# Causal attention on one core: the transfers of a group's load are issued by GpSimd between the masks of the second and third chunk, and the values have their own semaphore

## The reference

```python
xn = _layernorm(x, axis=-1)
s = _L0_attn_ref(xn, Wq, bq, Wk, bk, Wv, bv, Wo, bo)      # causal attention, the part changed here
g = _silu(_L0_ffn_ref(xn, ...))                           # two layers with windowed attention
x = x + s * g

# in _L0_attn_ref, for a chunk of queries qc of each head:
scores = jnp.einsum('bhqd,bhkd->bhqk', qc, k) * scale
scores = jnp.where(causal_mask[None, None], -jnp.inf, scores)
m = jnp.max(scores, axis=-1, keepdims=True)
p = jax.nn.softmax(scores - m, axis=-1)
oc = jnp.einsum('bhqk,bhkd->bhqd', p, v)
```

## Time and profile before

| | |
|---|---|
| time, median of 3 runs | 4990.12 us (4989.68 to 5007.07) |
| the profiled execution's own time | 4986.53 us |
| its span from first to last instruction | 4984.7 us |
| TensorE clock granted, mean | 0.949 of full speed |
| PE busy | 4590.0 us (92%) |
| DVE busy | 3673.8 us (74%) |
| ACT busy | 2994.0 us (60%) |
| POOL busy | 1342.6 us (27%) |

### The profile page before, as it was taken

How to read it: one execution, slowest core, us unless ns; L and a number is a source line. 1 busy time by engine, 2 the same in 40 slices (tenths; PEclk the granted TensorE clock), 3 DMA queues, 4 the chain that set the end, 5 groups by cost and what they waited for, 6 DMA issues and landing times. The chain is left out here.

```text
span 4984.7 us, 91933 instructions
## 1 busy us (share of the span) xinstructions
PE 4590.0 (92%) x32224; PEld 3005.9 (60%) x32224; DVE 3673.8 (74%) x7585; ACT 2994.0 (60%) x6873; POOL 1342.6 (27%) x1844
## 2 busy tenths in 40 slices
PE   8589999999999996899999999995999999999986
PEld 7433334333334332577777777764677777777766
DVE  7488887887878883777777777754777777777746
ACT  3157776777777774456565666651665656566642
POOL 3112111121111121433333333311433333333300
PEclk9789998999999997899999999996999999999998
DMA  8722432222432222000000000001000000000008
GB/s 300 212 34 35 57 45 36 36 35 41 55 42 36 36 36 69 5 9 18 10 18 10 14 13 14 14 9 65 5 18 10 18 10 18 10 14 14 14 6 277
DMA packets 174917, 214.21 MB, mean 43 GB/s; under 512 B 75068, under 2 KB 126228, under 8 KB 168340
## 3 DMA queue, kind: packets, MB, share of 16 engines
q1 hardware_dynamic: 174484, 208.56, 18.4%
HBM read 124.05 MB, written 83.89 MB: 42 GB/s over the span
## 5 line engine op out<-in xcount | busy, mean ns | idle before, releaser
L601 ACT ACTIVATE a_pt<-a_ring 128x512 f32<-128x512 f32 (+3 forms) x2560 | 1182.8, 542 | 474.4 <-PE a_ring L712 458.8
L652 DVE TENSOR_REDUCE a_mx<-a_ring 128x2 f32<-128x1024 f32 (+3 forms) x1092 | 1129.6, 1064 | 267.9 <-PE a_ring L732 164.3
L996 POOL TENSOR_TENSOR l_rn<-l_ssm,l_half 128x8 f32<-128x8 f32 x256 | 431.7, 1687 | 941.0 <-DVE l_ssm L1278 941.0
L725 PE MATMUL a_ring<-a_ks,a_qs 48*128 48x512 f32 (+3 forms) x2560 | 568.3, 439 | 115.7 <-DMA a_v_in<-v_d 83.1
L712 PE MATMUL a_ring<-a_qs,a_ks 49*128 49x512 f32 (+3 forms) x2560 | 574.3, 456 | 50.8 <-ACT a_pt L601 26.9
L749 PE MATMUL a_ot<-a_pt,a_vt 128*32 128x512 f32 (+3 forms) x5120 | 613.0, 559 | 1.8 <-ACT a_os L607 1.3
L712 PEld LDWEIGHTS a_ring<-a_qs,a_ks 49*128 49x128 f32 x2560 | 255.1, 193 | 454.9 <-ACT a_pt L601 271.8
L1097 ACT ACTIVATE l_pr<-l_pr,l_negm 128x256 f32<-128x256 f32 (+1 forms) x1024 | 501.8, 495 | 6.5 <-DVE l_negm L1330 6.1
L725 PEld LDWEIGHTS a_ring<-a_ks,a_qs 48*128 48x128 f32 x2560 | 265.9, 196 | 380.4 <-ACT a_pt L601 175.7
L575 POOL TENSOR_TENSOR a_gate<-a_gate 128x1 f32<-128x1 f32 x512 | 99.6, 195 | 1413.6 <-ACT a_pt L601 1403.4
L1003 POOL TENSOR_TENSOR l_work<-l_work,l_rot 128x512 f32<-128x512 f32 x256 | 357.4, 1397 | 396.0 <-DVE l_work L1286 396.0
(11 more groups left out here) (173 smaller groups left out, 9070.4 us busy)
## 6 DMA issues: line engine op xcount, KB each, us to landing
qk_d<-p_parts SPq DMA_DIRECT2D x16, 2048.0 KB, 10.4
a_qs<-qk_d SPq DMA_DIRECT2D x96, 256.0 KB, 8.5
a_ks<-qk_d SPq DMA_DIRECT2D x96, 256.0 KB, 18.5
x_d<-l_dx SPq DMA_DIRECT2D x32, 512.0 KB, 2.8
l_xt<-x_d SPq DMA_DIRECT2D x24, 513.0 KB, 3.8
p_x_in<-x SPq DMA_DIRECT2D x16, 512.0 KB, 8.8
x_d<-p_xt SPq DMA_DIRECT2D x16, 512.0 KB, 5.1
v_d<-p_vt SPq DMA_DIRECT2D x16, 512.0 KB, 10.8
```

The source lines that it names most:

```text
L601: act.activation(pt[:, (g * STEPS + s) % NPT, 2 * piece + f, q0:CHUNK], bank("step", g, k, f)[:, q0:CHUNK], ACT.Exp).then_inc(exp_done.sem, 1)
L652: r = dve.tensor_reduce(mx[:, pr, :, t, kc], ring[:, banks[0]:banks[1] + 1, 0:w], AX.X, ALU.max)
L725: mm = pe.matmul(bank("unit", G, n, f)[:, 0:w], qs[rows, v, pr, q0:q0 + P], ks[rows, v, pr, kc * CHUNK:kc * CHUNK + w], start=True, stop=k ...
L996: pool.tensor_tensor(out=rn[:, a * HEADS:(a + 1) * HEADS], in0=ssm[:, a * HEADS:(a + 1) * HEADS], in1=half[:, 0:HEADS], op=ALU.pow).then_i ...
```

## The change

GpSimd issues the 13 transfers instead of SP. They stand in its order between `step` 23 and `step` 24, that is behind the last mask of the second chunk. The transfer into `a_v_in` gets a semaphore of its own, `v_loaded`, for which only `widen` waits; `loaded` now counts the 12 transfers of queries and keys, and PE waits for those alone.

```diff
-        loaded = [tally(f"loaded{u}", 16 * (4 * NSTACK + 1)) for u in range(NSLOT)]
+        loaded = [tally(f"loaded{u}", 16 * 4 * NSTACK) for u in range(NSLOT)]
+        v_loaded = [tally(f"v_loaded{u}", 16) for u in range(NSLOT)]
...
         @block.sync
...
-            def load(G, _):
-                v, b, hg = G % NSLOT, G // NGROUP, G % NGROUP
-                sp.wait_ge(pv_done.sem, pv_done.at(G - NSLOT))
-                for dst, pick, o in ((qs, STACK_Q, 0), (ks, STACK_K, NGROUP)):
-                    for j, s in enumerate(pick):
-                        for f in range(2):
-                            row = f * HALF + j * A_HD
-                            sp.dma_start(dst[row:row + A_HD, v].bitcast(F32), parts_v[s, f, :, hg + o, :, b])\
-                              .then_inc(loaded[v].sem, 16)
-                sp.dma_start(v_in[:, v], v_v[:, b, hg]).then_inc(loaded[v].sem, 16)
...
-                do("row_out", 1); do("row_out", 2); do("load", 1); do("out", -1); do("out", 0); do("row_out", 3)
+                do("row_out", 1); do("row_out", 2); do("out", -1); do("out", 0); do("row_out", 3)
...
         @block.gpsimd
...
+            def load(G, _):
+                v, b, hg = G % NSLOT, G // NGROUP, G % NGROUP
+                pool.wait_ge(pv_done.sem, pv_done.at(G - NSLOT))
+                for dst, pick, o in ((qs, STACK_Q, 0), (ks, STACK_K, NGROUP)):
+                    for j, s in enumerate(pick):
+                        for f in range(2):
+                            row = f * HALF + j * A_HD
+                            pool.dma_start(dst[row:row + A_HD, v].bitcast(F32), parts_v[s, f, :, hg + o, :, b])\
+                              .then_inc(loaded[v].sem, 16)
+                pool.dma_start(v_in[:, v], v_v[:, b, hg]).then_inc(v_loaded[v].sem, 16)
+
             def widen(G, _):
                 v = G % NSLOT
-                pool.wait_ge(loaded[v].sem, loaded[v].per * (G // NSLOT + 1))
+                pool.wait_ge(v_loaded[v].sem, v_loaded[v].per * (G // NSLOT + 1))
...
-                for n in range(0, 49):
+                for n in range(0, 24):
+                    do("step", n)
+                do("load", 1)
+                for n in range(24, 49):
                     do("step", n)
                 do("widen", 1)
```

More of the change, by code:

```diff
@@ L542, in around @@
             def around(do):
-                do("row_out", 1); do("row_out", 2); do("load", 1); do("out", -1); do("out", 0); do("row_out", 3)
+                do("row_out", 1); do("row_out", 2); do("out", -1); do("out", 0); do("row_out", 3)
                 do("row_out", 4); do("out", 1); do("out", 2)
-            program(dict(load=load, row_out=row_out, out=out), around)
+            program(dict(row_out=row_out, out=out), around)
             for t in o_stored:
@@ L585, in around @@
                     do("step", n)
-            program(dict(widen=widen, step=step), around)
+            program(dict(load=load, widen=widen, step=step), around)
         @block.scalar
```

## The result

| | before | changed |
|---|---|---|
| median of 4 runs each | 4994.2 us (4989.7 to 5007.1) | 5184.4 us (5178.7 to 5190.4) |
| ratio, 95% interval | | 1.0386 [1.0361, 1.0411] |
| span of the profiled execution | 4984.7 us | 5188.4 us |
| mean granted clock | 0.949 | 0.930 |

A forecast was written before the change was run, and what follows sets the result against it. PE was taken to bound `attend`, busy 98.7 of 105.3 us a group. Fifteen groups each 12.5 us longer, 187 us, less 10 at the start, gave 177 us more: 5165 us, range 5080 to 5290.

The forecast's parts named there:

- The moved start: In each group the load starts behind GpSimd's last mask of the second chunk, 14.7 us later; the deciding term.
- The wait: PE, free 12.5 us behind the mask, waits 15.7 us for queries and keys landing 28.2 us behind it, 15 groups.
- The price of 1 us: Extra time until queries and keys land because GpSimd issues instead of SP: 1 us, added to 27.2 us.
- The fit in the Trainium skill: By it all 12 transfers need about 9 us, PE never waits, kernel gets faster; 129 GB/s spoke against it.
- The work of a group: A group in `attend` without its wait for the load takes 102.1 us; with the wait 117.8, against 105.3 before.
- the third rival: PE's clock stays low behind the long wait in every group, 8 us each: 120 us on top, 5285 us; 7%.
- The start: First load of the stage starts earlier from GpSimd and PE's first unit needs no values: 10 us gained.
- The sum: 15 x (102.1 + 15.7 - 105.3) - 10 = 177 us slower over the whole kernel.
- What was removed: PE's wait for values at each load, 2.1 us for each of 15 groups, nearly all of it to go.
- The masks: GpSimd's third-chunk masks stand behind the 13 issues; some 40 us of cover, so nothing counted for lateness.

The follow-up runs named there:

- sp_late: Kernel before, SP still issuing, but only after the second chunk's last mask, values on their own semaphore: 5177.1 us, ratio 1.0404 to the kernel before.
- pool_sync: Changed kernel with GpSimd's load behind step 7's mask, also waiting for the third chunk's maxima as SP did before: 4923.7 us, 0.9895 of the kernel before.
- split: Changed kernel with SP issuing the transfers into the upper 64 partitions, GpSimd the lower ones and the values: 5156.1 us, ratio 1.0359 to the kernel before.
- sp_vsem: Kernel before, SP issuing at the same place, only the values given their own semaphore: 4926.7 us, ratio 0.9902 to the kernel before.
- pool_mid: Changed kernel with the load four steps earlier in GpSimd's order, behind step 19: 5105.1 us, ratio 1.0264 to the kernel before.
- sp_first: Kernel before with values on their own semaphore and SP's first load ahead of constants and ones: 4935.1 us, ratio 0.9922 to the kernel before.
- warm: Changed kernel with 84 overwritten matmuls on PE ahead of its wait for each load but the first: 5184.9 us, ratio 1.0427 to the kernel before.

## Why the prediction was right

**The moved start** is shown as the cause: sp_late has the whole loss without GpSimd, pool_sync has none of it with GpSimd.

**The wait.** 15.7 us a group were forecast and 15.1 measured (226.4 / 15). The landing 28.2 us behind the mask was 28.5 in the load shown; PE came 12.5 us behind it or, where its clock had been low just ahead, up to 1.5 later, which shortens the wait. That the 28.2 came out is in part luck. It was 27.2 from one load plus 1 for the issuer, but that load was a quick one: over the 15 loads behind the first, queries and keys take 27.9 us on average before (25.2 to 29.0) and 28.1 in the changed kernel (27.6 to 28.7). The price of 1 us isn't there; with SP at the same mask (sp_late) they take 27.6, with GpSimd at SP's place (pool_sync) 27.5. GpSimd's issue costs 0.5 us, and the issues stay hidden, as said.

The Trainium skill (DMA: Bandwidth & Descriptors, Issuing engines are not separate DMA queues) says that transfers from different issuers share the same 16 DMA engines and interleave. The 126 to 129 GB/s of split and the averages of 27.9 and 28.1 us agree.

The fit in the Trainium skill (DMA: Bandwidth & Descriptors, Anatomy of one DMA) of 2 us plus the bytes at 436 GB/s, weighed in the prediction, is stated for one DMA. The 9 us that it gave for all twelve taken together were an estimate; the 27.6 to 28.7 us measured are three times that.

**The work of a group** was the mis-sized term. I took 102.1 us, the average of the stretches that began with a short low clock. Measured are 118.5 - 15.1 = 103.4. Ten of the 14 stretches are as forecast (118.30 less the next wait of 16.19 is 102.1); four take 120 to 121 with a mean clock of 0.87 to 0.88, so 121.00 - 14.41 = 106.6. In these the clock comes back 16 us behind the wait and not 8. The second 8 us behind two waits, an ordinary one and a long one:

```profile
689.50:697.50 8.00, 6.95 (x58) 3.29 (x57) 6.63 (x11) 6.77 (x14) 1.70 (x6) 1.00 0.00 1
...
807.40:815.40 8.00, 8.00 (x44) 3.76 (x42) 4.38 (x7) 4.63 (x9) 0.55 (x2) 0.50 0.00 0
```

That is the third rival in four groups at half its price. With it the average is 1.3 us over the forecast, 1.3 x 15 = 20 us. Why the clock stays low longer in four groups is open.

**The start** gave 9.1 us instead of 10: the first unit is at 218.75 and not 227.86.

```profile
218.75 0.48 PE L729 MATMUL a_ring<-a_ks,a_qs 48*128 48x128 f32 x2 [43.34 <-DMA a_ks<-a_ones]
```

PE waited for the ones, which took 20.0 us to land beside the load, as feared. The load itself landed less than 1 us ahead of them, 30.2 us behind its first issue at 187.8.

**The sum:** 177 + 20 for the work, 9 less for the wait, 1 more for the start are 189; measured were 190. So the time was closer than its terms, of which two were off in opposite directions.

**What was removed** I valued at the 2.1 us that PE waited. sp_vsem shows some 47 us for the 15 groups, 3.1 each. The sum hid this, because the long wait that takes its place has the same low clock behind it.

**The masks** of the third chunk weren't late, as forecast: PE waits once for POOL in the whole stage, for 0.5 us. In pool_mid, where the issues stand between masks of one chunk, they did.

## What to carry to other kernels

A load that moves to another engine moves to another place in time. Ask first which event it now follows, and when the one who needs it arrives: here 14.7 us of start became 13 us of wait in each group, and the issuer itself was worth nothing. Look at what else such an order kept apart: starting earlier than before let tiny stores run beside a 3.5 MB load, and PE waited 57 us for them. The short waits of a busy TensorE were worth nearly twice their length here, so a semaphore that counts only what is needed is a cheap thing to try alone.

## What the runs showed of the hardware

- An issue of these 256 KB transfers costs GpSimd 0.50 us (2.99 for 6) and SP 0.45 to 0.67 (2.69 for 6 in sp_first, 4.03 in sp_vsem); the one with 2048 runs of 256 bytes costs GpSimd 1.19 us and SP 0.43.
- Twelve of them into 16 partitions each take 27.9 us on average from SP (before) and 28.1 from GpSimd (after).
- Stores of 8 KB from one partition, issued by SP while a load from GpSimd fills the DMA engines, landed after 20.0 us (after); with no load beside them they took 1.9 (before).
- SP was held 20.3 us (sp_first) and 19.9 us (sp_late) in an issue behind 13 transfers of its own.
- Two queues with 16 partitions each from different halves move 126 to 129 GB/s (split), as one queue does.
- The low clock behind a wait of 3 us lasts about as long as behind one of 15 (granted 0.59 and 0.52 in the 8 us behind, warm and after), and filling four fifths of the wait with matmuls doesn't change the time (5177.7 against 5172.8 us).
